# A transformer block on one core: weight loads moved to SP's queue behind the first inputs, and a new order of steps on five engines

## The reference

```python
x = L0_attn_x                                      # (16, 256, 128)
x = x + layernorm(attn(layernorm(x), w_qkv, w_out))  # 16 heads of 8, softmax(q k^T / sqrt(128)) v
x = x + layernorm(ffn(layernorm(x), Wr, Wg, Wu, Wd, Sg, Su, Sd, bias))
# ffn: logits = x Wr + bias; top 2 of 8 experts, softmax over the two;
#      sum over experts of rw * (silu(x Wg) * (x Wu)) Wd, plus a shared expert with Sg, Su, Sd
```

## Time and profile before

| | us |
|---|---|
| median of 3 runs | 380.06 (378.44 to 380.81) |
| span of the profiled execution, first to last instruction | 378.7 |
| PE, DVE, ACT, POOL busy | 359.4, 310.7, 267.4, 200.8 |

### The profile page before, as it was taken

How to read it: one execution, slowest core, us unless ns; L and a number is a source line. 1 busy time by engine, 2 the same in 40 slices (tenths; PEclk the granted TensorE clock), 3 DMA queues, 4 the chain that set the end, 5 groups by cost and what they waited for, 6 DMA issues and landing times.

```text
span 378.7 us, 10110 instructions
## 1 busy us (share of the span) xinstructions
PE 359.4 (95%) x3342; PEld 231.8 (61%) x3342; DVE 310.7 (82%) x788; ACT 267.4 (71%) x511; POOL 200.8 (53%) x518
## 2 busy tenths in 40 slices
PE   7898799999999999999999999999999999999992
PEld 7866556455465557575657565665665566677872
DVE  8476579989899998989998889999998896767461
ACT  4563368788977877887878877786868876964522
POOL 5723121615556374848472835674744655858644
PEclk9999899999999999999999999999999999999998
DMA  2139766847534728557616937544773042222201
GB/s 76 44 105 150 180 123 131 183 140 153 148 105 137 181 54 205 142 144 174 140 58 165 230 103 182 132 121 121 161 181 113 7 115 74 85 74 69 71 8 38
DMA packets 59922, 45.65 MB, mean 121 GB/s; under 512 B 8966, under 2 KB 56966, under 8 KB 59870
## 3 DMA queue, kind: packets, MB, share of 16 engines
q1 hardware_dynamic: 56638, 44.02, 46.5%
q10 hardware_dynamic: 3232, 0.99, 2.3%
HBM read 26.69 MB, written 17.81 MB: 118 GB/s over the span
## 4 chain that ended last, share of the span: by engine, by line
PE 61%; issue 10%; POOL 7%; DMA 6%; DVE 6%; ACT 4%; SPq 3%; ACTq 1%; POOLq 0%; DVEq 0%
PE pvp L674 13%; PE sc L643 8%; PE sc L658 8%; PE bank_d L824 7%; PE bank_d L840 6%; PE bank_d L825 5%; PE bank_d L681 3%; PE bank_a L726 3%; DVE mx L1036 3%; DMA pv_dram<-pv_sb 2%; POOL rstd L1178 2%; POOL hidden L1245 2%; PE bank_d L797 2%; PE bank_a L735 2%; DMA ks<-qk_dram 1%
## 5 line engine op out<-in xcount | busy, mean ns | idle before, releaser
L1036 DVE TENSOR_REDUCE mx<-sc 128x4 f32<-128x1024 f32 x128 | 153.9, 1220 | 20.3 <-PE sc L643 19.4
L888 ACT ACTIVATE pr<-sc 128x1024 f32<-128x1024 f32 x128 | 129.8, 1024 | 32.8 <-PE sc L658 32.3
L674 PE MATMUL pvp<-pr,va 128*32 128x256 f32 x1024 | 68.5, 385 | 0.0
L824 PE MATMUL bank_d<-x3T,wg_sb 128*128 128x256 f32 x160 | 54.8, 424 | 1.3 <-DVE hidden L1134 1.2
L658 PE MATMUL sc<-qs,ks 51*128 51x256 bf16 x512 | 48.8, 274 | 4.1 <-DMA qs<-mT 2.0
L643 PE MATMUL sc<-ks,qs 48*128 48x256 bf16 x512 | 48.9, 274 | 1.1 <-DVE mx L1036 0.7
L1173 POOL TENSOR_TENSOR vareps<-mv,eps 128x2 f32<-128x2 f32 x64 | 12.6, 197 | 67.0 <-DVE mv L1028 67.0
L825 PE MATMUL bank_d<-x3T,wu_sb 128*128 128x256 f32 x160 | 47.6, 379 | 0.0
L1245 POOL TENSOR_TENSOR hidden<-hidden,rwb 128x256 f32<-128x256 f32 x60 | 43.0, 731 | 6.6 <-DMA rwb<-rw_dram 6.3
L1178 POOL TENSOR_TENSOR rstd<-vareps,mhalf 128x2 f32<-128x2 f32 x64 | 44.5, 696 | 0.0
L971 ACT ACTIVATE th<-bank_d 128x256 f32<-128x256 f32 x80 | 30.7, 384 | 18.4 <-PE bank_d L825 16.7
(11 more groups left out here) (113 smaller groups left out, 503.9 us busy)
## 6 DMA issues: line engine op xcount, KB each, us to landing
rwb<-rw_dram SPq DMA_DIRECT2D x30, 256.0 KB, 4.3
qk_dram<-parts SPq DMA_DIRECT2D x30, 192.0 KB, 3.4
qs<-qk_dram SPq DMA_DIRECT2D x30, 192.0 KB, 4.5
ks<-qk_dram SPq DMA_DIRECT2D x30, 192.0 KB, 5.1
qk_dram<-parts SPq DMA_DIRECT2D x30, 128.0 KB, 3.0
pv_dram<-pv_sb SPq DMA_DIRECT2D x14, 256.0 KB, 2.8
x_sb<-in_L_attn_x_dram SPq DMA_DIRECT2D x16, 128.0 KB, 3.0
out_dram<-x SPq DMA_DIRECT2D x16, 128.0 KB, 1.8
```

Of the source, the lines that this page charges most:

```text
L674: mm = pe.matmul(pvp[32 * j:32 * j + 32, g, :], values[:, X * c + 4 * g + j, 32 * tt:32 * tt + 32], pr[:, k, c * N:(c + 1) * N], start=(tt ...
L824: pe.matmul(bank_d[bank][:, 0:N], wg_sb[:, ORDER[n], :], x3T[b % 2][:], start=True, stop=True)
L888: nc.scalar.activation(pr[:, 2 * s:2 * s + 2, :].rearrange("p k n -> p (k n)"), sc[PAIR["s2", b, s]][:].rearrange("p u c n -> p (u c n)"), ...
L1036: nc.vector.tensor_reduce(mx[b % 2][:, :, :, s].rearrange("p c u -> p u c"), sc[PAIR["s1", b, s]][:], AX.X, ALU.max).then_inc(max_done, 1)
```

## The change

**The loads.** `load_wgu` and `load_wd` are now in SP's program. SP issues x0, w_qkv, x1, x2, x3, `load_wout` (8 DMAs), `load_wgu` (7), x4, `load_wd` (3), then `spill.1`, x5, `stack.1`, `spill.2`, `load_minus`, `max_stack.0`. Before, `max_stack.0` stood ahead of `spill.2`, behind `stack.1` and `load_minus`.

**The order.** All tables are new. The ticks are now mere ranks from 0 to 1910. The heads of the orders, as the tables give them:

- DVE before: the copies for `lay_steps(0)`, `rw` memsets, `va0, stats1.0, aggr1.0, wv, wqk, stats1.1, aggr1.1, va1, stats1.2, ...`; after: `lay0a, lay0b, rwz, stats1.0, aggr1.0, stats1.1, va1, wqk, aggr1.1, va0, wv, stats1.2, aggr1.2, rest1.0, ...`; and `rest1.2` now stands between `max_3.0` and `max_4.0`, `rest1.3` behind `max_7.0` as before.
- ACT before, behind `v_copy.0`: `apply1.2, apply1.3, xT_copy.1, kh_copy, part1.1, kl_copy`; after: `apply1.2, xT_copy.1, kh_copy, part1.1, kl_copy, part2.1, xT_copy.2, qh_copy, part1.2, apply1.3, part2.2, v_copy.1, xT_copy.3, part1.3, max_copy.0, v_copy.2, ...`.
- PE up to `s2_0.0` has the same steps but for `xT.4`, which comes just behind it now. In all of PE's order the spacing stays alike: between `maxT` and `s2_0` of one batch lie steps of PE of a similar length.
- At the end PE had `gu3.15, gu4.15, wsel, down.14, down.15` and has `gu3.15, wsel, gu4.15, down.14, down.15`; ACT had `down_copy.14, apply4.14, down_copy.15, apply4.15` and has `down_copy.14, down_copy.15, apply4.14, apply4.15`.

**Fillers.** 39 instead of 89 in FILL, 8 instead of 14 in FILL_LAST.

**Waits.** `sel1` waits no longer for all eight of ACT's copies of `lay_steps(1)` and `(2)`; `sel2` and `sel3` wait for their own. `v` waits for `xT_copied` itself, since it need not follow `qk` in the new order.

The diff, cut to what the text speaks of:

```diff
 TIMES = {
-    "load_x": [0, 48, 72, 98, 374, 549, 685, 1177, 1999, 2024, 2677, 2901, 3867, 5052, 5971, 7954],
...
-    "load_wgu": [1289],
...
-    "load_wd": [1677],
...
+    "load_x": [0, 12, 14, 15, 48, 80, 119, 129, 131, 133, 222, 260, 282, 437, 516, 801],
+    "lay0a": [1],
+    "lay0b": [2],
+    "rwz": [3],
+    "lay1": [4],
+    "lay2": [5],
...
+    "load_wout": [17],
...
+    "load_wgu": [33],
...
+    "load_wd": [53],
...
 FILL = {
-    "maxT": {0: 10, 1: 1}, "proj": {0: 2}, "qk": {0: 2, 1: 2, 2: 1}, "s1_2": {1: 2, 2: 1}, "s1_3": {1: 3},
-    "s1_4": {0: 2, 1: 3}, "s1_5": {3: 1}, "s1_6": {0: 3, 3: 2}, "s1_7": {0: 3, 1: 1}, "s2_0": {1: 5},
-    "s2_1": {1: 2}, "s2_4": {0: 3, 1: 2}, "s2_5": {0: 2, 1: 2}, "sel1": {0: 3}, "v": {1: 1},
-    "xT": {0: 24, 3: 5, 4: 1},
+    "maxT": {0: 9},
+    "qk": {0: 1},
+    "s1_3": {0: 2},
+    "s1_4": {0: 2, 1: 1},
+    "s1_5": {0: 2, 2: 1},
+    "s2_0": {0: 2},
+    "s2_4": {0: 2, 1: 1},
+    "s2_5": {0: 1},
+    "sel1": {0: 2},
+    "xT": {0: 12, 3: 1},
 }
 FILL_LAST = {
-    "down": {15: 2}, "gu0": {15: 1}, "gu2": {14: 1, 15: 1}, "gu3": {14: 1, 15: 1}, "gu4": {14: 3},
-    "router": {14: 2, 15: 2},
+    "down": {15: 6},
+    "router": {14: 1, 15: 1},
 }
@@ sync @@
+            def load_wgu():
+                sp.dma_start(wr_sb[:], Wr).then_inc(wgu_load, DMA)
+                sp.dma_start(wg_sb[:, 4, :], Sg).then_inc(wgu_load, DMA)
+                sp.dma_start(wu_sb[:, 4, :], Su).then_inc(wgu_load, DMA)
+                for e2 in range(2):
+                    es = slice(4 * e2, 4 * e2 + 4)
+                    half = slice(F * e2, F * e2 + F)
+                    sp.dma_start(wg_sb[:, 0:4, half], Wg[es].rearrange("c d f -> d c f")).then_inc(wgu_load, DMA)
+                    sp.dma_start(wu_sb[:, 0:4, half], Wu[es].rearrange("c d f -> d c f")).then_inc(wgu_load, DMA)
...
             for tick in TICKS:
+                if due(tick, "load_wgu") == 0:
+                    load_wgu()
+                if due(tick, "load_wd") == 0:
+                    load_wd()
@@ tensor @@
+                    pe.wait_ge(xT_copied, b + 1)
                     turn(a_empty)
...
                         if n == 0:
                             pe.wait_ge(lay_done0, 6)
-                            pe.wait_ge(lay_done, 8)
+                        else:
+                            pe.wait_ge(lay_done, 4 * n)
@@ scalar @@
-            act.wait_ge(identb_done, 1)
-            act.wait_ge(lay_zeroed, 1)
-            for n in (1, 2):
-                for src, dst in lay_steps(n):
-                    nc.scalar.copy(dst, src).then_inc(lay_done, 1)
-
             for tick in TICKS:
-                if due(tick, "load_wgu") == 0:
-                    load_wgu()
-                if due(tick, "load_wd") == 0:
-                    load_wd()
+                for n in (1, 2):
+                    if due(tick, f"lay{n}") is not None:
...
@@ vector @@
             for tick in TICKS:
+                for n in range(2):
+                    if due(tick, f"lay0{'ab'[n]}") is not None:
...
+                if due(tick, "rwz") is not None:
+                    for r in range(2):
+                        nc.vector.memset(rw[r][:, TT * E:], 0.0).then_inc(rw_zeroed, 1)
```

More of the change, by code:

```diff
@@ L59 @@
[L59 to L63, removed]
[3 rows of a table removed]
-    "spill": [None, 1022, 1667, 2234, 2746, 3159, 4124, 5500, 6543, 7245, 8021, 9449, 10051, 10987, 12057, 12945],
-    "qh_copy": [1029],
[6 rows of a table removed]
-    "stack": [None, 1258, 1904, 2582, 3064, 3892, 5077, 5876, 6780, 7859, 8562, 9769, 10775, 11234, 12723, 13209],
-    "max_4": [1266, 1862, 2546, 3330, 4154, 4960, 5989, 6758, 7801, 8677, 9743, 10804, 11592, 12564, 13508, 14586],
-    "s1_5": [1277, 1943, 2575, 3341, 4219, 5046, 6055, 6822, 7864, 8799, 9840, 10794, 11654, 12641, 13555, 14621],
@@ L230 @@
[L230 to L236, removed]
+    "load_x": [0, 12, 14, 15, 48, 80, 119, 129, 131, 133, 222, 260, 282, 437, 516, 801],
[4 more added lines that the diff above has]
+    "lay2": [5],
+    "stats1": [16, 19, 31, 39, 102, 104, 152, 163, 172, 227, 365, 453, 494, 542, 672, 951],
@@ new lines @@
+    "load_wout": [17],
+    "aggr1": [18, 24, 34, 41, 103, 108, 162, 211, 236, 335, 441, 492, 541, 598, 772, 958],
+    "rstd1": [20, 27, 37, 57, 106, 113, 168, 213, 240, 347, 443, 590, 612, 838, 899, 963],
+    "va1": [21],
+    "apply1": [22, 35, 46, 75, 116, 122, 189, 253, 277, 429, 501, 632, 778, 915, 1003, 1164],
+    "wqk": [23],
+    "va0": [25],
+    "xT": [26, 49, 63, 90, 128, 199, 272, 388, 475, 616, 738, 863, 957, 1079, 1216, 1323],
+    "xT_copy": [28, 52, 65, 92, 134, 203, 274, 393, 480, 619, 749, 867, 971, 1094, 1223, 1332],
@@ new lines @@
+    "qk": [29, 54, 70, 94, 137, 206, 280, 410, 503, 642, 753, 869, 979, 1104, 1228, 1346],
+    "wv": [30],
+    "part1": [32, 58, 74, 97, 156, 215, 284, 424, 534, 655, 759, 874, 994, 1110, 1234, 1361],
+    "load_wgu": [33],
[6 rows of a table added]
+    "v_copy": [45, 88, 115, 121, 183, 263, 377, 444, 605, 705, 794, 928, 1033, 1142, 1271, 1395],
+    "pickm": [47],
+    "minusm": [50],
+    "sel3": [51],
+    "load_wd": [53],
+    "ql_copy": [55],
+    "kh_copy": [56],
+    "selq": [59],
+    "kl_copy": [60],
+    "s1_0": [64, 107, 165, 229, 283, 391, 493, 607, 700, 831, 932, 1069, 1179, 1290, 1386, 1515],
@@ new lines @@
+    "load_minus": [101],
+    "maxT": [105, 186, 265, 300, 397, 488, 609, 718, 834, 942, 1065, 1201, 1288, 1419, 1503, 1619],
+    "max_copy": [109, 188, 266, 306, 402, 499, 613, 732, 839, 947, 1071, 1206, 1298, 1424, 1505, 1622],
+    "max_stack": [112, 190, 270, 309, 409, 509, 615, 736, 843, 965, 1077, 1210, 1315, 1430, 1509, 1627],
[20 rows of a table added]
+    "pv_copy": [184, 269, 344, 426, 537, 643, 757, 912, 1011, 1123, 1219, 1337, 1459, 1555, 1667, 1769],
+    "osel": [193, None, None, None, None, None, None, None, None, None, None, None, None, None, None, 1773],
@@ L237 @@
+    "down_copy": [469, 676, 803, 901, 1019, 1131, 1260, 1374, 1458, 1581, 1652, 1730, 1796, 1850, 1893, 1901],
[5 rows of a table added]
+    "store": [628, 790, 923, 1025, 1107, 1229, 1329, 1486, 1571, 1657, 1727, 1791, 1858, 1882, 1908, 1910],
+    "wsel": [1876],
+    "hwl0": [1892],
+    "hwl1": [1894],
+    "hwl2": [1895],
+    "hwl3": [1896],
 }
 FILL = {
[4 rows of a table removed]
+    "maxT": {0: 9},
[5 more added lines that the diff above has]
+    "s2_4": {0: 2, 1: 1},
@@ L536, in load_bias, with load_wd @@
                 sp.dma_start(bias_sb[:], src).then_inc(bias_load, DMA)
+            def load_wgu():
[7 more added lines that the diff above has]
+                    sp.dma_start(wu_sb[:, 0:4, half], Wu[es].rearrange("c d f -> d c f")).then_inc(wgu_load, DMA)
+            def load_wd():
+                sp.dma_start(wd_sb[:, 4, :], Sd).then_inc(wd_load, DMA)
+                for e2 in range(2):
+                    es = slice(4 * e2, 4 * e2 + 4)
+                    sp.dma_start(wd_sb[F * e2:F * e2 + F, 0:4, :], Wd[es].rearrange("c f d -> f c d")).then_inc(wd_load, DMA)
             load_x(0)
@@ L995, in _ @@
             nc.vector.memset(lay_words[:, 0:X * WIDTH], 0.0).then_inc(lay_zeroed0, 1)
-            dve.wait_ge(identb_done, 1)
-            dve.wait_ge(lay_zeroed0, 1)
-            for src, dst in lay_steps(0):
-                nc.vector.tensor_copy(dst, src).then_inc(lay_done0, 1)
-            for r in range(2):
-                nc.vector.memset(rw[r][:, TT * E:], 0.0).then_inc(rw_zeroed, 1)
             def permute_qk():
```

177 lines of the change are left out of this document (37 added, 140 removed), and 134 rows, old and new, of the table TIMES.

## The result

The changed kernel takes 377.79 us in the median (372.97 to 381.55, 20 runs); the kernel before, in runs beside it, takes 379.09 us (377.72 to 381.83, 20 runs). The ratio is 0.995, with a 95% interval of 0.993 to 0.997. The interval leaves out 1, so there is a gain, but a small one: 1.3 us between the medians, a third of the 1% that the prediction took as what can be told apart, where it said 9.4 us; the time is just outside its range. The profiled execution spans 376.6 us, 2.1 less than the one of before. Both run lists spread over 4 us and more, and the mean granted clock of the changed kernel's runs over 0.976 to 0.998.

The account below looks back on a forecast made before the run. PE was taken as the bound from 80 to 345 us, so gains had to come from the head: -6.0 to `s2_0.0`, -1.7, -2.5, 0 and +0.8 gave -9.4 us. Forecast 371.0 us, range 365.5 to 377.5.

Parts of the forecast that it names:

- (a): DVE's head: `stats1.0` ahead of `va0` brings the first steps, up to `xT.0`, forward; taken as -1.4 us.
- (b): ACT from `xT.0` to `s1_0.0`: `apply1.3` moves behind the copies it stood ahead of; taken as -0.9 us.
- (c): Maxima up to `maxT.0`: `part1.3` no longer waits on ACT, so `maxT` follows its input closely; -1.7 us.
- (e): SP's queue ahead of `max_stack.0`: early weight loads lose nothing, `spill.2` and `load_minus` cost little; taken as +0.2 us.
- (d): Landing of batch 0's maxima before `s2_0.0`: faster with the weights no longer in flight; taken as -2.2 us.
- (f): Behind `s2_0.0`: the half-clock spell from 42 to 45 us goes if PE has no such gap; -1.7 us.
- (g): Behind `s2_0.0`: 6 fillers instead of 27 free PE time, half of it counted; -2.5 us.
- (j): Head: fewer fillers make the clock less sure, half a spell of 3.4 us at half clock; +0.8 us.
- (h): From 80 to 345 us: same steps, neighbours alike, so no change; taken as 0, between -2 and +3 us.
- Rival 2: The clock: longer PE idling puts most of the head at half clock, three spells costing 5.1 us; 376 us, 14%.
- Rival 3: Slower: a step placed ahead of its input stops its engine once per batch in the saturated stretch; 388 us, 7%.
- Rival 1: The head gains but DVE's backlog of maxima takes it back before 80 us; 374.9 us or nearer 377, 14%.

Follow-up runs that it names:

- 2: The changed kernel with the six stores of `spill.2` issued behind `max_stack.0` on SP: 378.3 us, ratio 0.995.
- Kernel 1: The kernel before with only the weight loads moved to SP and issued early, its order and all fillers kept: 375.42 us, ratio 0.991.
- Kernel 7: The changed kernel with the ten loads of the wgu and wd weights issued by ACT again: 383.61 us, ratio 1.013.
- 3: The changed kernel with 27 fillers put back in the head, 66 instead of 39: 376.32 us, ratio 0.993.
- 4: The changed kernel's order up to `gu0.0`, then the order of the kernel before with its 14 last fillers: 374.94 us, ratio 0.989.
- 5: The changed head with the old order behind `gu0.0`, `spill.2` behind `max_stack.0` and 27 fillers put back in the head: 374.74 us, ratio 0.992.
- 8: The changed kernel with 27 head fillers put back, `spill.2` behind `max_stack.0` and `spill.11` behind `max_stack.9`: 375.96 us, ratio 0.997.
- Kernel 9: The kernel before, unchanged, timed and profiled a second time as a kernel of its own: 378.64 us, ratio 1.003.
- 6: The kernel before with only its table of head fillers replaced by the changed kernel's, 39 instead of 89: 381.69 us, ratio 1.010.
- 10: The kernel before with early loads on SP up to `gu0.0`, then the changed kernel's order: 379.28 us, ratio 1.000.
- 11: Kernel 8 with `down.5`, `down.8` and `down.12` later on PE and `w_load.6` ahead of `spill.13` on SP: 384.82 us, ratio 1.016.

## Why the prediction was wrong, step by step

In the profiles the time went from 378.7 to 376.6 us, 2.1 instead of 9.4. Of the 7.3 us between them the way to `s2_0.0` lacks 2.5 (3.5 us for 6.0), the way from there to `gu0.0` 3.1 (0.3 us for 3.4), and the way from `gu0.0` to `down.15` 2.4; the tail gave 0.6 that was not forecast.

**Steps (a), (b), (c): right in their sum, in part by luck.** Together they should bring `maxT.0` forward by 1.4 + 0.9 + 1.7 = 4.0 us, and it went from 35.30 to 31.28. (a) gave 1.9 (`xT.0` at 7.6). (b) gave nothing in the profiled execution, since `qk.0` ran at half clock and took 1.81 us, but 2, which has the same order and kept its clock there, has `s1_0.0` at 18.0 instead of 19.3. The stretch behind it, where (c) lies, gave 2.1 instead of 1.7. Kernel 1 shows ACT's part alone: `maxT.0` at 34.1, 1.2 us earlier, with no change in the order.

**Step (e) failed: "`max_stack.0` now has `spill.2` and `load_minus` ahead of it ... I take +0.2".** To the end of the two issues it measured +2.2: 0.7 for SP not free and 1.5 because the two issues took 2.97 us behind eight others. I counted the issues as time on SP at a fixed length; kernel 2, with the stores moved away, has 1.48. Step (d), the landing at -2.2, was near: 1.7 in the changed kernel (35.66 to 38.10 is 2.44 against 4.15), and none of it waited for in 1 and 2. Kernel 7, with the weights in flight again, has 4.7. The sum had one more gap: it let `s2_0.0` follow the maxima alone. In 2, 3, 4, 5 and 8 it waits for no DMA and starts at 36.1 to 36.9, behind PE's own steps and fillers since `maxT.0`; no term stood for them. So the DMA wait behind (e) was 1.6 us at most, and 35.6 was not reached with it taken away.

**Step (f) failed: "-1.7 if `s2_0.0` starts without such a gap".** A spell of one execution was booked as a property of the kernel. Kernel 9 has none at 42 us. The changed kernel lost the clock there all the same, for 3.4 us from 39.55, which the step had named as the case in which it is worth 0. The base of the sum, 380.1, was itself 1.0 us above the later median of 20 runs (379.09), and the profile a long one (9 spans 375.8), so the changed kernel's profile, with 376.6, is 2.1 us shorter than one profile of the kernel before and 0.8 longer than the other.

**Step (g) failed, with its sign: "Behind `s2_0.0` stood 27 fillers, now 6 ... -2.5".** From `s2_0.0` to `gu0.0` the kernel before takes 38.1 us (with its spell of 1.7) and 36.6 in 9; kernels 1, 3 and 5, with fillers, 36.9, 36.2 and 36.7; the changed kernel 37.7 and kernel 4 38.5. So taking the fillers out brought nothing forward: PE's idle time from 41.6 to 80 us went from 0.3 us to 3.5, and the clock from 0.96 to 0.94 (1.00 in 9). Step (j) had the clock's part at +0.8; 6 has 3.7 us for fillers and clock together in the old order. In the changed kernel less of it reaches the end (3 against the change: 0.2% between the ratios); why is not shown.

**Step (h) failed: "the same steps, neighbours alike; taken as 0, between -2 and +3".** From `gu0.0` to `down.15` the kernel before takes 289.3 us, 9 288.3, 1 288.2 and 4 288.8. The changed kernel takes 291.7, 3 290.5, 8 292.4 and 10 295.1. The profiles give +2.4 here, and all seven with the new order there (290.5 and more) lie above all six with the old one (5, with 290.0, is the longest). By the ratios it is 0.5 to 0.9%. It took 2.4 of the 3.9 us that the head had gained. PE's waits for 80 to 345 us in the changed kernel:

```profile
PE bank_d L818 <- POOL hidden L1206: 1.7, 4, 0.6
PE sc L632 <- DMA qs<-mT: 1.7, 2, 1.4
PE bank_d L802 <- DVE hidden L1095: 1.2, 2, 0.9
PE sc L632 <- DVE mx L997: 0.7, 2, 0.5
PE bank_d L775 <- POOL on L1177: 0.7, 2, 0.5
```

In the kernel before the same view has 2.4 us for DVE's `mx` and 0.6 for all else. "PE waits that add up to over 5 us" was what the prediction named as a sign that it was wrong, and here they are.

**The rivals.** Rival 2, the clock, was near in time (376) and in its mechanism: three spells, and the Trainium skill's page cited there had the direction. Rival 3 is what (h) is, not once per batch but at a few places of 0.5 to 1.5 us. Rival 1 shows once the head is mended: in 5 DVE takes back 1.3 of the 1.7 us that are lost against kernel 1 behind `gu0.0`. None of the three is the whole account. Step (i), taken as 0, was right within 0.6 us: `down.15` to the end took 9.7 us before and 9.1 after.

What the change is made of, then: loads off ACT and early, -0.9% by 1 (and by 7 some 1.7% within the new order); 50 fillers out, up to +1.0% by 6; the new head's order, nothing beyond 1 that reaches the end, by 4 and 5; the new order behind 80 us, +0.5 to +0.9% by 4, 8 and 10. These are differences between kernels and need not add up. Kernels 1, 4 and 5 have lower ratios than the change, at 0.989 to 0.992, and their intervals overlap, so no best one of them is told. Kernel 1 needs eighteen moved issues and no new order.

What stays open is which property of the new order makes it short of slack behind 80 us. Mending the SP queue alone (8) did not cure it, and moving single steps (11) made it worse; an order of its own for SP was not tried.

## What to carry to other kernels

When a change bundles a move with a new order, try the move alone first: here it held the whole gain. Dummy matmuls that look like free PE time may be what keeps the clock; before counting them as gain, see what the engine would do in their place. On an in-order queue a small transfer behind bulk ones is issued late, by 4.5 us in one batch of the changed kernel; before moving it, see whether the engine that wants it would be free sooner, since in 2 and 8 the move cured the delay and no time came of it. And take the profile of the kernel before twice before pricing any single spell or wait in it.
